# Two graph layers on one core: the setup before the attention loop, put in a new order, with part of it moved to GpSimd and TensorE

## The reference, cut to what matters

```python
h = relu(layernorm(x))
x = x + deg * (h @ Wi.T + b) + adj @ (h @ Wj.T)          # first layer, W = [Wi | Wj]
h = relu(layernorm(x))                                   # here: x1
# four heads; W_heads: 4 x 256 x 256, a_heads: 4 x 512
Wh = h @ W_heads;  f1 = Wh . a[:256];  f2 = Wh . a[256:]
e  = leaky_relu(f1[i] + f2[j], 0.01);  e = where(adj > 0, e, -1e9)
h  = elu(softmax(e) @ Wh)                                # heads side by side: 1024 wide
# the same once more with one head (W_out: 1024 x 256, a_out: 512), then elu
y  = relu(out @ w1 + b1) @ w2 + b2 + out
x  = x + layernorm(y) * gamma + beta
```

## Time and profile before

| | |
|---|---|
| median of 3 runs | 1696.31 us (1692.17 to 1696.42) |
| profiled execution: time, span | 1692.9 us, 1691.1 us |
| busy: TensorE, DVE, ACT, GpSimd | 1564.2, 1456.0, 1377.5, 1001.9 us |
| mean granted TensorE clock | 0.978 of full |
| setup, up to the first masked row | about 84 us |

### The profile page before, as it was taken

How to read it: one execution, slowest core, us unless ns; L and a number is a source line. 1 busy time by engine, 2 the same in 40 slices (tenths; PEclk the granted TensorE clock), 3 DMA queues, 4 the chain that set the end, 5 groups by cost and what they waited for, 6 DMA issues and landing times.

```text
span 1691.1 us, 36352 instructions
## 1 busy us (share of the span) xinstructions
PE 1564.2 (92%) x13183; PEld 1315.1 (78%) x13184; DVE 1456.0 (86%) x2526; ACT 1377.5 (81%) x1862; POOL 1001.9 (59%) x1428
## 2 busy tenths in 40 slices
PE   5448999999999999999999999999999999998997
PEld 3336878788787887788787887878877888887876
DVE  4877699879999798988999799997989889898876
ACT  4177599879988798878997799887998789989972
POOL 4065367447675566656676476755766566686532
PEclk9779999999999999999999999999999999999999
DMA  8356498749987599767987599876998689788845
GB/s 267 75 139 112 101 199 156 121 90 188 186 147 115 122 182 173 131 101 159 206 139 123 97 189 184 145 116 124 183 173 129 101 138 184 123 134 131 136 76 100
DMA packets 780082, 240.87 MB, mean 142 GB/s; under 512 B 746624, under 2 KB 773376, under 8 KB 779776
## 3 DMA queue, kind: packets, MB, share of 16 engines
q1 hardware_dynamic: 772064, 231.18, 73.9%
q0 software_dynamic: 7840, 7.37, 3.8%
HBM read 38.01 MB, written 15.89 MB: 32 GB/s over the span
## 4 chain that ended last, share of the span: by engine, by line
PE 57%; DVE 13%; ACT 8%; issue 7%; DMA 6%; POOL 5%; SPq 3%; DVEq 0%; ACTq 0%; POOLq 0%
PE ps L130 10%; PE ps L1395 9%; PE ps L1401 9%; PE ps L1396 9%; PE ps L1415 6%; PE ps L139 5%; PE ps L1428 4%; DVE p_lo L1123 4%; PE ps L1476 2%; DMA pt_hi<-p_hi 2%; ACT p_hi L994 2%; DMA cat<-f_rows 2%; ACT xr L981 2%; DVE xr L1116 2%; SPq L860 2%
## 5 line engine op out<-in xcount | busy, mean ns | idle before, releaser
L1395 PE MATMUL ps<-pt_hi,hv_hi 128*128 128x256 f16 x2048 | 465.0, 274 | 33.3 <-DMA pt_hi<-p_hi 33.2
L1396 PE MATMUL ps<-pt_hi,hv_lo 128*128 128x256 f16 x2048 | 464.9, 274 | 0.0
L1123 DVE SCALAR_TENSOR_TENSOR p_lo<-xr,rden,p_hi 128x1024 f16<-128x1024 f32 x320 | 412.8, 1290 | 31.6 <-ACT p_hi L994 29.6
L994 ACT ACTIVATE p_hi<-xr,rden 128x1024 f16<-128x1024 f32 x320 | 366.6, 1146 | 39.3 <-POOL rden L903 37.9
L987 ACT ACTIVATE xr<-xr,shift 128x1024 f32<-128x1024 f32 x320 | 366.8, 1146 | 3.2 <-POOL shift L916 3.2
L901 POOL TENSOR_SCALAR den<-sums 128x1 f32<-128x1 f32 x320 | 154.3, 482 | 362.8 <-ACT xr L987 360.9
L1116 DVE CUSTOM_DVE_ANT_0 xr<-cat,mask_add 128x1024 f32<-128x1024 f32 x256 | 311.6, 1218 | 7.9 <-DMA cat<-f_rows 7.9
L981 ACT ACTIVATE xr<-xr,f1h 128x1024 f32<-128x1024 f32 x256 | 292.9, 1145 | 5.5 <-DVE mx L1116 5.5
L903 POOL TENSOR_TENSOR rden<-den,minus_one 128x1 f32<-128x1 f32 x320 | 265.2, 829 | 26.7
L1401 PE MATMUL ps<-pt_lo,hv_hi 128*128 128x256 f16 x2048 | 267.4, 274 | 1.7 <-DMA pt_lo<-p_lo 1.5
L914 POOL TENSOR_SCALAR zt<-mx,f1h 128x1 f32<-128x1 f32 x256 | 192.9, 754 | 115.5 <-DVE mx L1116 112.6
(11 more groups left out here) (199 smaller groups left out, 3126.8 us busy)
## 6 DMA issues: line engine op xcount, KB each, us to landing
cat<-f_rows SPq DMA_DIRECT2D x32, 512.0 KB, 4.5
out<-xx SPq DMA_DIRECT2D x28, 256.0 KB, 2.5
xx<-in_x SPq DMA_DIRECT2D x28, 256.0 KB, 3.4
out<-fin POOLq DMA_DIRECT2D x28, 256.0 KB, 5.3
pt_hi<-p_hi SPq DMA_TRANSPOSE x320, 3.3
pt_lo<-p_lo SPq DMA_TRANSPOSE x320, 3.3
adj_i<-in_adj SPq DMA_DIRECT2D x4, 1024.0 KB, 11.8
f2o<-f2o_rows SPq DMA_DIRECT2D x7, 512.0 KB, 4.2
```

Of the source, the lines that this page charges most:

```text
L994: nc.scalar.activation(p_hi[:, k % P_SLOTS, :], xr[:, k % X_SLOTS, :], ACT.Copy, scale=rden[:, k % 8:k % 8 + 1]).then_inc(hi_done, 1)
L1123: nc.vector.scalar_tensor_tensor(p_lo[:, k % P_SLOTS, :], xr[:, k % X_SLOTS, :], rden[:, k % 8:k % 8 + 1], p_hi[:, k % P_SLOTS, :], ALU.mu ...
L1395: nc.tensor.matmul(to, vh, hi, start=t == 0, stop=False)
L1396: nc.tensor.matmul(to, vl, hi, start=False, stop=False)
```

## The change

All of it lies in the setup and in the first units of the main loop.

- x1 is normalised in halves: `means_of` and `rsqrt` run once for each half, four columns wide.
- The first four units read the f2 rows from PSUM: TensorE multiplies a column of the identity, spread over 128 columns, with `rows0`, which puts one head's row on every partition (head 0 in psC, head 1 in psA). `cat` is loaded after the setup block.
- The second layer's folds become two full-width products on GpSimd (`wo_by_a`) and two sums on DVE; GpSimd also makes the scaled `whf` and its low part, which DVE made before.
- All nine scales come from one chain (`half_exponents`, then `sc`), after one wait.
- The loads of `ah_bc` and `wof` change places; the folds of the heads are partly placed between the `m_low`; `mask_add` stands before `m_low(0)`; the saves of x1 stand behind the transposes; `wo_hi` stands between the two high parts of x1, and `wo_lo` is made in two halves around the second `low`.

```diff
@@ SP, setup
-                    sp.dma_start(wof[:, :, :], w_out.rearrange("(k p) n -> p k n", p=P)).then_inc(w_in, DMA)
-                    sp.dma_start(ah_bc[:, :, :, :].rearrange("p h c f -> p (h c f)"), a_heads.rearrange("h c -> (h c)").partition_broadcast(P)).then_inc(a_in, DMA)
-                    sp.dma_start(ao_bc[:, :, :].rearrange("p c f -> p (c f)"), a_out.partition_broadcast(P)).then_inc(a_in, DMA)
+                    sp.dma_start(ah_bc[:, :, :, :].rearrange("p h c f -> p (h c f)"), a_heads.rearrange("h c -> (h c)").partition_broadcast(P)).then_inc(ah_in, DMA)
+                    sp.dma_start(wof[:, :, :], w_out.rearrange("(k p) n -> p k n", p=P)).then_inc(wo_in, DMA)
+                    sp.dma_start(ao_bc[:, :, :].rearrange("p c f -> p (c f)"), a_out.partition_broadcast(P)).then_inc(wo_in, DMA)
...
                     for i in range(2):
                         turn(LN_X1, hv_hi[0], hv_lo[0], i, h1T_in)
+                        for u in (2 * i, 2 * i + 1):
+                            sp.wait_ge(x10_done, i + 1)
...
-                    sp.wait_ge(f2_saved, 4 * DMA)
-                    for m in range(H):
-                        load_row(sp, 0, m)
@@ GpSimd, setup
-                    pool.wait_ge(w_in, 3 * DMA)
+                    pool.wait_ge(w_in, 2 * DMA)
                     nc.gpsimd.tensor_tensor(sq[:, :], whf_flat, whf_flat, ALU.mult).then_inc(sq_done, 1)
+                    pool.wait_ge(wo_in, 2 * DMA)
                     nc.gpsimd.tensor_tensor(sqo[:, :], wof_flat, wof_flat, ALU.mult).then_inc(sq_done, 1)
-                    rsqrt(LN_X1)
+                    pool.wait_ge(adj16_done, T)
+                    for c in range(2):
+                        nc.gpsimd.tensor_tensor(wo_by_a[c], wof[:, :, :], ao_bc[:, c, :].unsqueeze(1).to_broadcast([P, KH, F]), ALU.mult).then_inc(by_a_done, 1)
+                    rsqrt(LN_X1, 1, slice(0, half))
+                    pool.wait_ge(sc_done, 1)
+                    nc.gpsimd.tensor_scalar(wh_scaled, whf_flat, scale(S_WH), None, ALU.mult).then_inc(wh_scaled_done, 1)
+                    rsqrt(LN_X1, 2, slice(half, T))
+                    pool.wait_ge(wh_scaled_done, 1)
+                    pool.wait_ge(whi_done, 2)
+                    nc.gpsimd.tensor_tensor(wh_lo[:, :, 0:HF], wh_scaled.rearrange("p (k n) -> p k n", k=KF), wh_hi[:, :, 0:HF], ALU.subtract).then_inc(whlo_done, 1)
+                    pool.wait_ge(whlo_done, 1)
@@ ACT, setup
                     high(LN_X1, hv_hi[0], 0)
+                    nc.scalar.activation(wo_hi[:, :, 0:F], wof[:, :, :], ACT.Copy, scale=scale(S_WO)).then_inc(whi_done, 1)
+                    nc.scalar.activation(wo_hi[:, :, F:V], wao[:, :, :], ACT.Copy, scale=scale(S_WAO)).then_inc(whi_done, 1)
                     high(LN_X1, hv_hi[0], 1)
@@ DVE, setup
+                    def fold_out(c):
+                        dve.wait_ge(by_a_done, c + 1)
+                        link(nc.vector.reduce_sum(wao[:, :, c], wo_by_a[c], axis=AX))
...
+                    nc.vector.tensor_scalar(mask_add[:, :], adj16[:, :, :].rearrange("p t j -> p (t j)"), 0.0, MASKED, ALU.is_le, ALU.mult)
                     m_low(0)
                     m_low(1)
+                    dve.wait_ge(w_in, 2 * DMA)
+                    dve.wait_ge(ah_in, DMA)
+                    fold_heads(0, 2)
                     m_low(2)
+                    fold_heads(2, 4)
                     m_low(3)
-                    fold_heads(0)
-                    fold_heads(1)
-                    nc.vector.tensor_tensor(sqa[:, 0:16], waf_flat, waf_flat, ALU.mult).then_inc(sqa_done, 1)
+                    fold_heads(4, 16)
+                    nc.vector.tensor_tensor(sqa[:, 0:16], waf_flat, waf_flat, ALU.mult)
+                    fold_out(0)
+                    fold_out(1)
+                    nc.vector.tensor_tensor(sqa[:, 16:32], wao_flat, wao_flat, ALU.mult).then_inc(sqa_done, 1)
                     x1_out(0)
+                    means_of(LN_X1, 1, range(half))
...
+                    split_low(waf[...], wh_hi[...], wh_lo[...], S_WA, 1).then_inc(wa_done, 1)
+                    normalise(LN_X1, 0)
+                    x1_out(1)
+                    means_of(LN_X1, 2, range(half, T))
+                    low(LN_X1, hv_hi[0], hv_lo[0], 0)
+                    normalise(LN_X1, 1)
+                    split_low(wof[:, 0:KH // 2, :], wo_hi[:, 0:KH // 2, 0:F], wo_lo[:, 0:KH // 2, 0:F], S_WO, 3)
+                    low(LN_X1, hv_hi[0], hv_lo[0], 1)
+                    split_low(wof[:, KH // 2:KH, :], wo_hi[:, KH // 2:KH, 0:F], wo_lo[:, KH // 2:KH, 0:F], S_WO, 3)
+                    split_low(wao[:, :, :], wo_hi[:, :, F:V], wo_lo[:, :, F:V], S_WAO, 4)
                     dve.wait_ge(f10_ps, 1)
                     nc.vector.tensor_copy(*first_scores(psD, f1h[0])).then_inc(f1_done, 1)
@@ TensorE, setup: one wait for all squares, ahead of the second neighbour product; then
                     pe.wait_ge(rows_done, 1)
+                    for m, spread in enumerate((psC, psA)):
+                        for q in range(4):
+                            row = 32 * q + H + m
+                            last = nc.tensor.matmul(spread[:, q * 2 * P:(q + 1) * 2 * P], ident[:, row:row + 1].to_broadcast([P, P]), rows0[:, :], start=True, stop=True)
+                        last.then_inc(f2_first, 1)
                     pe.wait_ge(x10_done, 2)
                     scores_T(psD, rows0).then_inc(f10_ps, 1)
@@ main loop: SP begins with
+            sp.wait_ge(f2_saved, 4 * DMA)
+            for m in range(H):
+                load_row(sp, 0, m)
@@ main loop, DVE, masked_row
+                first_rows = layer == 1 and b == 0 and i < 4
+                if first_rows:
+                    hold(dve, "dve", f2_first, m + 1)
@@ main loop, TensorE, attend
+                if j == 0:
+                    pe.wait_ge(x_done, 4)
```

More of the change, by code:

```diff
@@ L207, in build @@
             wof_flat = wof[:, :, :].rearrange("p k f -> p (k f)")
+            spare = adj_i[:, :, :].rearrange("p t j -> p (t j)").bitcast(F32)
+            wh_scaled = spare[:, 0:KF * HF]
+            wo_by_a = [spare[:, (1 + c) * KF * HF:(2 + c) * KF * HF].rearrange("p (k f) -> p k f", f=F) for c in range(2)]
             waf_flat = waf[:, :, :, :].rearrange("p k c h -> p (k c h)")
@@ L282, in _, with rsqrt @@
                 def _(pool):
[L283 to L289, removed]
+                    def rsqrt(i, count, tiles):
+                        hold(pool, "pool", mv_done[i], count)
+                        part = rstd[:, tiles]
+                        nc.gpsimd.tensor_scalar(part, mv[:, tiles, 1], LN_EPS, None, ALU.add).then_inc(eps_done[i], 1)
+                        pool.wait_ge(eps_done[i], count)
+                        nc.gpsimd.tensor_tensor(part, part, half_neg[:, tiles], ALU.pow).then_inc(pow_done[i], 1)
+                        hold(pool, "pool", pow_done[i], count)
+                        nc.gpsimd.tensor_scalar(part, part, LN_SCALE, None, ALU.mult).then_inc(rstd_done[i], 1)
                     chain = [0]
@@ L391, in stats_of, with means_of @@
                             last = nc.vector.bn_stats(stats[:, t, :], xx[:, t, :])
[L392 to L397, removed]
+                        last.then_inc(stats_done[i], 1)
+                    def means_of(i, ready, tiles):
+                        hold(dve, "dve", stats_done[i], ready)
+                        for t in tiles:
                             last = nc.vector.bn_aggr(mv[:, t, :], stats[:, t, :])
@@ L440, in fold, with fold_heads @@
                         link(nc.vector.tensor_tensor_reduce(out=junk[:, :], in0=w, in1=a, scale=1.0, scalar=0.0, op0=ALU.mult, op1=ALU.add, accum_out=to))
[L442 to L447, removed]
-                        for i in range(a, b):
-                            c, k = i // KH, i % KH
-                            fold(wao[:, k, c:c + 1], wof[:, k, :], ao_bc[:, c, :])
+                    def fold_heads(a, b):
+                        for i in range(a, b):
+                            c, k, h = i // (KF * H), i // H % KF, i % H
+                            fold(waf[:, k, c, h:h + 1], whf[:, k, h, :], ah_bc[:, h, c, :])
+                    def fold_out(c):
+                        dve.wait_ge(by_a_done, c + 1)
+                        link(nc.vector.reduce_sum(wao[:, :, c], wo_by_a[c], axis=AX))
                     def split_low(src, hi, lo, s, i):
@@ L518, in _ @@
                     nc.vector.tensor_scalar(ebits[:, S_H:S_H + 1], kf[:, 0:1], -1.0, 254.0 + WH_LOG, ALU.mult, ALU.add)
-                    link(nc.vector.tensor_scalar(ebits[:, S_HINV:S_HINV + 1], kf[:, 0:1], -float(LN_LOG + W_LOG), None, ALU.add))
-                    powers(0, 5, 1)
-                    split_low(waf[:, :, :, :].rearrange("p k c h -> p k (c h)"), wh_hi[:, :, HF:HF + NF], wh_lo[:, :, HF:HF + NF], S_WA, 1).then_inc(wa_done, 1)
-                    fold_out(0, 5)
-                    x1_out(1)
@@ L547, in _ @@
```

(1 more changed line is left out.)

82 lines of the change are left out of this document (31 added, 51 removed).

## The result

The changed kernel takes 1709.2 us (median of 4 runs, 1707.34 to 1710.82). The kernel before, run beside it, takes 1695.37 us (4 runs). The ratio is 1.0084, 95% interval 1.0066 to 1.0103. The forecast was 1707.9 us, in its likeliest case: full-width GpSimd work that makes DVE wait.

The account below looks back on a forecast made before the run. A chain of small setup steps, mostly DVE, sets when the first masked row starts: 14.1 us later, less 2.5 for faster filling, gives +11.6 on 1696.3, so 1707.9 us. Own range 1704 to 1714; overall from 1689.5 to 1714.5.

Parts of the forecast that it names:

- likeliest case: Setup: full-width GpSimd work makes two-tile DVE instructions wait, 11.6 us slower in all; chance 0.62.
- Price of a full-width product: Setup, GpSimd: each wo_by_a product of two tiles over 2048 elements takes 4.3 us, between 3.6 and 5.7.
- A DVE instruction on two tiles stands still for the whole of a long one: Setup: a two-tile DVE instruction such as a fold waits out a whole GpSimd instruction; rows showed this for 512 elements only.
- m_low(3) as the step through which it costs: Setup, DVE: folds waiting for GpSimd put m_low(3)'s end at 52.5 instead of 42.8, 9.7 us on the path.
- wh_scaled, one tile: Setup, GpSimd: scaling whf takes 2.5 us, between half of 3.60 and 3.60, and holds wa_lo until 72.3.
- normalise runs at its usual speed beside GpSimd: Setup, DVE: normalise(0) takes 1.35 us; normalise(1) proceeds while GpSimd runs wh_lo until 83.4.
- rstd of half the width: Setup, GpSimd: rstd for one half of x1 takes 2.3 us, from 76.8 to 79.1.
- Spreading and end of the block: Setup's end: TensorE products, turn of the rows and copy of f1 take 6.6 us, bounds 4.4 and 8.2.
- the third case: The fast case, in which the time falls below what can be told from no change; chance 0.12.
- Faster filling: Main loop's start: first masked rows read PSUM, so GpSimd's first shift takes 0.29 instead of 2.17 us; gain 2.5 us.
- The rule for a late cat: First units: masked row 4 waits for cat; each microsecond its load is more than half a microsecond late costs one.
- The rival in which long GpSimd instructions don't hold DVE up: Setup: the port is free or costs little beside full-width GpSimd work; chance 0.26.

Follow-up runs that it names:

- the folds moved: The changed kernel with all 16 folds of the heads behind m_low(3), not four of them between the m_low: 1707.56 us, ratio 1.0077.
- the two products alone: The kernel before plus two full-width GpSimd products behind sqo (wof by the halves of a_out) that nobody reads: 1701.55 us, ratio 1.0037.
- no GpSimd work: The changed kernel with second-layer folds and whf's low part on DVE, and all head folds behind m_low(3): 1695.03 us, ratio 1.0004.
- The kernel made late: The kernel before with mask_add computed eight times instead of once, which only starts the main loop late: 1711.59 us, ratio 1.0098.

## Why the prediction was right, and where its steps were off

Its place and its cause held, and its sum came near. One step failed, and two errors partly cancel in the time (below). Against its own steps:

- **Price of a full-width product: 4.3 us** (bounds 3.6 and 5.7). Measured 4.68 each where a fold stands ahead of it, and 4.51 and 4.52 for the first product in the two kernels where none does (the folds moved; the two products alone). The 4.3 was an estimate drawn through the rows at 256 and 512 elements, and is 0.2 to 0.4 short.
- **A DVE instruction on two tiles stands still for the whole of a long one.** The rows of before showed it at 512 elements; for longer ones it was the prediction's estimate. Right at 2048 elements too, in all seven long folds shown above, but not for wa_lo beside the scaling of whf, which got through 1.75 us before GpSimd was done. The order was right as well: fold, product, fold, product, with m_low(3) done at 51.8 (predicted 52.5), and squares of the folds at 62.1 (62.75).
- **m_low(3) as the step through which it costs.** Wrong as a reason, right in size. With m_low(3) early again only 1.0 us came back: the folds are needed just as much. Of 17.8 us of first row the runs give 5.4 to the new order, DVE's 16 second-layer folds ahead of the one exponent chain, and the half clock (no GpSimd work: 89.74, granted clock 0.50 from 80 to 88 us), 3.5 to the products and sums in place of DVE's folds (93.22), and 9.0 to whf's scaling and low part (102.18). The 3.5 is a difference: DVE is spared 16 folds of 0.466, 7.5 us, for two sums that take 4.6 together, and loses the rest in waits. The clock has a part in these shares: the spreading takes 6.66, 5.23 and 6.35 us in the three kernels, and counted at its start (82.16, 87.07, 94.91) the last two shares are 4.9 and 7.8.
- **wh_scaled, one tile: 2.5 us.** Mis-sized. It takes 5.46, outside the bounds (half of 3.60, and 3.60), longer than a product of two tiles. It held wa_lo until 73.0 (predicted 72.3) and then, not foreseen, the first normalise until about 74.8.
- **normalise runs at its usual speed beside GpSimd** (1.35 us for a half, and the second half done while wh_lo runs). This is the step that failed. Its first instance took 1.94 us beside wh_scaled and 4.17 beside wh_lo, against 0.40. The means were ready at 79.0 (predicted 76.8). The last low started at 88.3 and ended at 89.5 (85.9). Of these 3.6 us, 1.5 are the first normalise and about 1.0 the second, whose other three instances now stand behind wh_lo and not beside it. That a DVE instruction which reads a single SBUF tile is free to run was an assumption of mine: it held for m_low(2), 0.87 us beside the second product, and not for the normalise. Why, no row shows.
- **rstd of half the width: 2.3.** 2.9, from 79.0 to 81.9 (predicted 79.1). GpSimd's first instruction took 1.01 us where the same one of the first half took 0.24: it ended at 80.3, just behind the low of half 0 on DVE (79.04 to 80.23), which reads two SBUF tiles. So here GpSimd waited for DVE.
- **Landing of the transposes 3.85 us, scores 2.1.** 3.2 and 2.1.
- **Spreading and end of the block: 6.6 us** (bounds 4.4 and 8.2). 7.3, from 94.85 to 102.18. The clock stayed at half for the first 5 of the spreading's 6.35 us, 1.5 longer than taken. The clock also stayed at 0.50 through the score products, so what the third case (TensorE at full clock in the spreading) wanted did not happen.
- **First masked row 98.5.** 102.18: 3.7 late, of which 3.6 had gathered by low(1).
- **Faster filling: 2.5 us.** The shift at 104.07 takes 0.30, not the 2.17 of the earlier trace rows, and the first low part comes 8.25 us after the first row instead of 10.4: 2.2, and 2.5 at unit 1. The rule for a late cat held as well: the fifth masked row waits 2.43 us for it and ends 8.25 us behind the first one's start, not 7.4, so the low part that was due at 7.9 is 0.35 late.

The sum said +11.6 us and the medians say +13.8; the profiled pair says +17.9. The prediction's base was 0.9 above the median of the runs beside which the change was timed, so 1707.9 is nearer to 1709.2 than the sum deserved; that part is luck. From unit 1 the path is 15.3 us longer, 3.7 more than predicted, and the TensorE steps of the late kernels came on top in that execution, which the prediction did not have. The kernel made late pays 17.0 us in its medians for a shift of 16.5; the kernel after pays 13.8 for 15.3, and its profiled execution is the longest of its four. So a path that was 3.7 us too short in the prediction, and a main loop that gave part of it back in the medians, make up the near hit; where it gave it back was not looked at.

The rival in which long GpSimd instructions don't hold DVE up forecast 1693.3 (1691.5 to 1700); the kernel without the new GpSimd work takes 1695.03. The prediction speaks of a port, and no run shows one: they show that folds of 0.42 us took up to 4.61 beside full-width GpSimd products. The third case, the fast one, forecast 1690 and needed full clock in the spreading besides, which no kernel had that didn't add work for it.

## To carry to other kernels

Before moving work from DVE to an idle GpSimd, list what DVE does in those microseconds. Here a fold (two SBUF tiles, up to 4.61 us for 0.42) and a normalise (a tensor_scalar from SBUF to SBUF, up to 4.17 for 0.40) stood still for what was left of the GpSimd instruction, and on a chain every such wait counted in full. Look whether the moved work was hidden where it stood: here one DVE instruction of 2.35 us, off the path, became 8.4 us of waiting on it. Read the granted clock of the stretch before a detour through TensorE is priced: it was 0.50 here from 84 to 100 us, and the spreading took 6.35 us instead of 3.72.

## What the runs showed of the hardware

- A GpSimd tensor_scalar of 128x2048 f32 from one tile takes 5.46 us, in three kernels alike; a product of two such tiles 4.51 to 4.69, a difference of two with f16 output 4.05, a square with bf16 output 3.60 (5.07 beside mask_add, see the next point).
- GpSimd waited for a DVE tensor_scalar too, though that reads a single SBUF tile. In the kernel after, mask_add (28.89 to 31.18) overlaps the square of whf, which starts at 29.58 and takes 5.07 us; in the kernel before, where mask_add stands elsewhere, the same square takes 3.60. That is 1.47 us more for 1.60 of overlap. This cost nothing, since nobody waited for that square.
- Beside the GpSimd tensor_scalar of 5.46 us, wa_lo (two SBUF tiles) ended at 73.0, when 1.75 us of the GpSimd instruction were still to come, and the normalise behind it then waited until its end. In the kernel with the folds moved the same two take 3.40 and 2.90. So this one GpSimd instruction let a DVE one in; why, is open.
- A queued GpSimd and a queued DVE instruction took turns in the kernel after: the folds take 2.88, 4.59 and 3.20 us between sqo and two products, never one wait for all three.
- One and the same stretch of TensorE work, after the same idle 2.20 us, got a clock of 1.00 in the kernel before and of 0.57 in three later ones (after, the two products alone, and the one made late), one execution each: 1.7 us for one such step. What decides it is open.
